# A macaron FFN / Mamba / FFN layer: GpSimd work of the first FFN moved into its down phases, dt * A made by other engines, the short FFN chunk in two matmuls

## The reference, cut to what matters

```python
x = x + 0.5 * ffn(layernorm(x))       # x: (1, 2048, 256)
x = x + mamba(layernorm(x))
x = x + 0.5 * ffn(layernorm(x))       # the same FFN weights

def ffn(x):                           # weights: lut[idx], 16 values
    gate, up = x @ lut[gate_idx].T, x @ lut[up_idx].T     # 256 -> 688
    return (silu(gate) * up) @ lut[down_idx].T            # 688 -> 256

def mamba(h):
    proj = h @ in_proj_w * mup        # z 512, x 512, B 128, C 128, dt 64
    xBC = silu(causal_conv4(xBC) + conv_b)
    dt = softplus(dt + dt_bias)       # 64 heads
    A = -exp(A_log)
    dA = exp(dt * A)                  # the decay of one step
    # scan: state = state*dA + (dt*x) B^T ;  y = C state + D*x
    return (rms_norm(y) * norm_w * silu(z)) @ out_proj_w
```

## Time and profile before

| | |
|---|---|
| runs, us | 550.12, 551.39, 548.0 (median 550.12) |
| profiled execution, us | 552.35, of which the span is 550.6 |
| mean granted PE clock | 0.964 |
| PE busy | 483.1 us, 88% |
| DVE busy | 386.7 us, 70% |
| ACT busy | 280.1 us, 51% |
| POOL busy | 181.0 us, 33% |

### The profile page before, as it was taken

How to read it: one execution, slowest core, us unless ns; L and a number is a source line. 1 busy time by engine, 2 the same in 40 slices (tenths; PEclk the granted TensorE clock), 3 DMA queues, 4 the chain that set the end, 5 groups by cost and what they waited for, 6 DMA issues and landing times.

```text
span 550.6 us, 17195 instructions
## 1 busy us (share of the span) xinstructions
PE 483.1 (88%) x7502; PEld 403.0 (73%) x7502; DVE 386.7 (70%) x734; ACT 280.1 (51%) x506; POOL 181.0 (33%) x229
## 2 busy tenths in 40 slices
PE   4999997989999889548899999999877699999997
PEld 3657886969887678436677778777766678898986
DVE  6998747474749996983687888777758747465542
ACT  3667624232438778766555665556635433232231
POOL 1100006084022221084566667665646311000000
PEclk9999998999999999778899999999989999999999
DMA  9940150000000000010000000000250000101011
GB/s 209 241 166 1 80 245 2 1 1 1 0 1 0 2 0 1 0 38 23 4 4 5 4 5 5 4 4 5 83 249 4 2 3 0 39 1 38 1 39 39
DMA packets 7163, 21.34 MB, mean 39 GB/s; under 512 B 688, under 2 KB 5296, under 8 KB 6448
## 3 DMA queue, kind: packets, MB, share of 16 engines
q1 hardware_dynamic: 6688, 18.08, 9.9%
q10 hardware_dynamic: 400, 2.16, 1.7%
HBM read 12.90 MB, written 6.55 MB: 35 GB/s over the span
## 4 chain that ended last, share of the span: by engine, by line
PE 35%; issue 9%; POOL 5%; DVE 2%; ACT 1%; POOLq 0%; DVEq 0%; ACTq 0%
PE intra L940 4%; POOL w L1169 3%; PE seg L819 3%; PE yo L68 2%; PE yo L70 2%; PE yo L69 2%; PE new L914 2%; PE XB L902 2%; PE XB L873 1%; PE seg L814 1%; PE prior L909 1%; PE intra L68 1%; PE intra L69 1%; PE intra L70 1%; PE yo L889 1%
## 5 line engine op out<-in xcount | busy, mean ns | idle before, releaser
L495 POOL TENSOR_TENSOR n_rstd<-n_ve,m_half 128x4 f32<-128x4 f32 x12 | 13.7, 1145 | 165.6 <-DVE n_ve L491 165.6
L1169 POOL TENSOR_TENSOR w<-xdt,ends 32x512 f32<-32x512 f32 (+3 forms) x63 | 66.5, 1074 | 1.7 <-PE prior L909 1.5
L959 ACT ACTIVATE seg<-seg 128x512 f32<-128x512 f32 x64 | 35.9, 579 | 52.7 <-PE seg L819 52.6
L597 DVE SCALAR_TENSOR_TENSOR cv<-pre,vec,cv 128x512 f32<-128x512 f32 x72 | 59.9, 846 | 3.8 <-ACT cv L653 2.1
L1038 DVE TENSOR_TENSOR mmat<-seg,gs 128x512 f32<-128x512 f32 x64 | 42.5, 684 | 11.8 <-ACT seg L959 11.5
L979 ACT ACTIVATE xbd<-xdt 32x512 f32<-32x512 f32 x64 | 39.9, 624 | 1.2
L819 PEld LDWEIGHTS seg<-abk,m_seg 96*32 96x32 bf16 x2048 | 21.2, 98 | 25.0 <-DVE mmat L1038 14.0
L940 PE MATMUL intra<-xbd,mmat 128*32 128x32 f32 x2048 | 34.3, 223 | 5.0 <-issue 5.0
L940 PEld LDWEIGHTS intra<-xbd,mmat 128*32 128x32 f32 x2048 | 32.0, 152 | 7.8 <-issue 6.0
L68 PE MATMUL pj<-n_xT,win 128*128 128x512 f32 x88 | 35.8, 407 | 1.1 <-PEq L118 1.1
L819 PE MATMUL seg<-abk,m_seg 96*32 96x64 bf16 x2048 | 28.4, 197 | 8.9 <-issue 5.7
(11 more groups left out here) (228 smaller groups left out, 1453.4 us busy)
## 6 DMA issues: line engine op xcount, KB each, us to landing
wgu_dram<-wgu SPq DMA_DIRECT2D x1, 2816.0 KB, 8.2
wgu<-wgu_dram SPq DMA_DIRECT2D x1, 2816.0 KB, 10.5
out<-x_res SPq DMA_DIRECT2D x4, 512.0 KB, 2.9
x_res<-in_x SPq DMA_DIRECT2D x1, 1536.0 KB, 24.4
wd_dram<-wd SPq DMA_DIRECT2D x1, 1536.0 KB, 11.5
wd<-wd_dram SPq DMA_DIRECT2D x1, 1536.0 KB, 13.7
gu_idx<-in_gu ACTq DMA_DIRECT2D x4, 352.0 KB, 8.1
gu_idx<-in_gu SPq DMA_DIRECT2D x4, 352.0 KB, 12.6
```

The lines of the kernel that those rows point to most:

```text
L597: dve.scalar_tensor_tensor(dst, pre[:, x, k:k + GN].rearrange("p (t c) -> p t c", c=P), cw[:, x, k:k + 1], dst, ALU.mult, ALU.add).then_in ...
L959: act.activation(seg[u_ % 2][:, :, :], seg[u_ % 2][:, :, :], ACT.Exp).then_inc(s["exp_ok"], 1)
L1169: pool.tensor_tensor(heads(w[r, n, :]), heads(xdt[a % 2][r, :]), ends[a % 2][r, n * HEADS:(n + 1) * HEADS].unsqueeze(2) .broadcast_to([Q * ...
```

## The change

- `build_masks` no longer sets `m_seg` by a memset and six selections on 32 partitions each; it makes `below = 1 - tri` and one product of two broadcast tiles (96 x 1024).
- GpSimd's steps in the first FFN each wait for `h_lo` of a whole group: masks for group 0, the halves of `win` for groups 1 and 2, `wout` for group 3. The `n_rstd` stand between them.
- Chunk 5 has 48 rows; its low part now goes to partitions 64 to 111 of the high part's tile, and the down weights of chunk 5 stand twice, in both halves of the partitions. Two products per token tile do what three did, in both FFNs. One more copy of 64x256 fills the second half; one memset less clears `hT` and `wd`.
- In the projection's last group A stands by head (one column). ACT multiplies dt by it before the transposes; PE transposes both (16 instead of 8); ACT copies both out and makes the three bf16 parts; DVE makes the two differences. GpSimd has none of it. The softplus steps stand two convolution blocks later on DVE, and the transposes one bank later on PE.

```diff
-    pool.memset(m_seg[:, :, :], 1.0).then_inc(built, 1)
...
-        if b < PARTS:
-            pool.affine_select(out=m_seg[r, :, :], in_=m_seg[r, :, :], compare_op=ALU.is_gt, fill=0.0, base=0,
-                               pattern=[[0, Q], [-1, Q]], channel_multiplier=1).then_inc(built, 1)
...
-            n += 2
         pool.affine_select(out=tri[r, :], in_=tri[r, :], compare_op=ALU.is_ge, fill=0.0, base=0, pattern=[[1, Q]],
                            channel_multiplier=-1).then_inc(built, 1)
         pool.wait_ge(built, n + 1)
         n += 1
+    K = PARTS * Q
+    pool.tensor_scalar(below[:, :], tri[:, :], -1.0, 1.0, ALU.mult, ALU.add).then_inc(built, 1)
+    pool.wait_ge(built, n + 1)
+    pool.tensor_tensor(m_seg[:, :, :], tri[0:K, :].unsqueeze(2).broadcast_to([K, Q, Q]),
+                       below[0:K, :].unsqueeze(1).broadcast_to([K, Q, Q]), ALU.mult).then_inc(built, 1)
+    n += 2
...
+def low_part(hT, c, rows):
+    return hT[0:rows, 1, c, :] if c < FCH - 1 else hT[H64:H64 + rows, 0, c, :]
+def down_mm(pe, out, hT, wd, c, tok):
+    if c < FCH - 1:
+        return split_mm(pe, out, hT[:, 0, c, tok], hT[:, 1, c, tok], wd[:, 0, c, :], wd[:, 1, c, :], c == 0, False)
+    pe.matmul(out, hT[:, 0, c, tok], wd[:, 0, c, :], start=False, stop=False)
+    return pe.matmul(out, hT[:, 0, c, tok], wd[:, 1, c, :], start=False, stop=True)
...
-            for hl in range(2):
-                pool.memset(hT[:, hl, FCH - 1, :].bitcast(F32), 0.0).then_inc(hz, 1)
+            pool.memset(hT[:, 0, FCH - 1, :].bitcast(F32), 0.0).then_inc(hz, 1)
             norm.pool_rstd(pool, 1)
-            norm.pool_rstd(pool, 2)
+            pool.wait_ge(h_lo, FCH)
+            build_masks(pool, T, T["built"])
             for k in range(KC):
+                norm.pool_rstd(pool, k + 2)
+                pool.wait_ge(h_lo, (k + 2) * FCH)
                 pool.wait_ge(split_hi, k + 1)
                 for part in range(4):
                     c = slice(part * PCH * P // 4, (part + 1) * PCH * P // 4)
                     pool.tensor_tensor(win[:, 1, k, :, :].rearrange("p c n -> p (c n)")[:, c], win_raw[:, k, c],
                                        win[:, 0, k, :, :].rearrange("p c n -> p (c n)")[:, c].bitcast(F32), ALU.subtract)
-            norm.pool_rstd(pool, 3)
-            build_masks(pool, T, T["built"])
+            norm.pool_rstd(pool, GROUPS)
+            pool.wait_ge(h_lo, GROUPS * FCH)
             pool.wait_ge(split_hi, KC + 1)
             for k in range(4):
                 pool.tensor_tensor(wout[:, 1, k, :], wout_raw[:, k, :], wout[:, 0, k, :].bitcast(F32), ALU.subtract)
-            norm.pool_rstd(pool, GROUPS)
...
-                    dve.tensor_tensor(hT[0:r, 1, c, :], h[0:r, :], hT[0:r, 0, c, :].bitcast(F32),
+                    dve.tensor_tensor(low_part(hT, c, r), h[0:r, :], hT[0:r, 0, c, :].bitcast(F32),
                                       ALU.subtract).then_inc(h_lo, 1)
...
-                        for e in range(2 if d < FCH - 1 else 1):
-                            ins = act.activation(wd[H64 * e:H64 * e + H64, hl, d, :],
-                                                 down_bank(d)[half, HID * e:HID * e + HID], ACT.Copy)
+                        for e in range(2 if d < FCH - 1 else 2 - hl):
+                            at = HID * e if d < FCH - 1 else 0
+                            ins = act.activation(wd[H64 * e:H64 * e + H64, hl, d, :], down_bank(d)[half, at:at + HID], ACT.Copy)
...
-                    if not ahead and n == 0:
+                    if not ahead and n == 2:
                         dve.wait_ge(eA_ok, 1)
-                        dve.tensor_scalar(A_bc[:, :], A_bc[:, :], -1.0, None, ALU.mult).then_inc(A_ok, 1)
+                        dve.tensor_scalar(A_col[:, :], A_col[:, :], -1.0, None, ALU.mult).then_inc(A_ok, 1)
...
-                    if not ahead and n == 1:
+                    if not ahead and n == 3:
                         dve.wait_ge(nd_ok, 1)
                         dve.wait_ge(ln_ok, 1)
...
+                    if not ahead and n == 5:
+                        dve.wait_ge(hi_ok, 1)
+                        dve.tensor_tensor(rest[:, :], a_tok[:, :], part(0), ALU.subtract).then_inc(rest_ok, 1)
...
+            dve.wait_ge(hi_ok, 2)
+            dve.wait_ge(rest_ok, 1)
+            dve.tensor_tensor(rest[:, :], rest[:, :], part(1), ALU.subtract).then_inc(rest_ok, 1)
...
-            dt_flat = dt_tok[:, :, :].rearrange("p t h -> p (t h)")
-            part = lambda n: ab[:, n, :, :].rearrange("p t h -> p (t h)")
-            pool.wait_ge(dttok_ok, GROUPS)
-            pool.wait_ge(A_ok, 1)
-            pool.tensor_tensor(a_tok[:, :].rearrange("p (t h) -> p t h", h=HEADS), dt_tok[:, :, :],
-                               A_bc[:, :].unsqueeze(1).broadcast_to([P, TILES, HEADS]), ALU.mult).then_inc(a_ok, 1)
-            pool.wait_ge(a_ok, 1)
-            pool.tensor_copy(part(0), a_tok[:, :]).then_inc(hi_ok, 1)
-            pool.wait_ge(hi_ok, 1)
...
-            pool.wait_ge(rest_ok, 2)
-            pool.tensor_copy(part(2), rest[:, :]).then_inc(hi_ok, 1)
...
+                        if last:
+                            act.activation(e, raw, ACT.Abs).then_inc(abs_ok, 1)
                         if g:
                             silu(g - 1, XCH - 1)
-                        if last:
-                            act.activation(e, raw, ACT.Abs).then_inc(abs_ok, 1)
-                            act.wait_ge(abs_ok, 1)
-                            act.activation(e, e, ACT.Exp, scale=-1.0).then_inc(exp_ok, 1)
-                            act.activation(A_bc[:, :], T["a_row"][:, :], ACT.Exp).then_inc(eA_ok, 1)
                     if not last and place == TRANSPOSE_AT + 1:
                         norm.act_hi(act, g + 1)
-                    if last and place == 1:
+                    if last and place == 2:
+                        act.wait_ge(abs_ok, 1)
+                        act.activation(e, e, ACT.Exp, scale=-1.0).then_inc(exp_ok, 1)
+                        act.activation(A_col[:, :], T["a_col"], ACT.Exp).then_inc(eA_ok, 1)
+                    if last and place == 3:
                         act.wait_ge(u_ok, 1)
                         act.activation(ln[:, :], u[:, :], ACT.Ln).then_inc(ln_ok, 1)
+                    if last and place == 4:
+                        act.wait_ge(A_ok, 1)
+                        act.wait_ge(dt_ok, 1)
+                        act.activation(e, raw, ACT.Copy, scale=A_col[:, 0:1]).then_inc(by_head, 1)
                     if last and place == 5:
-                        act.wait_ge(tr_dt, 1)
-                        for q in range(GROUPS):
-                            act.activation(dt_tok[:, q * GT:q * GT + GT, :].rearrange("p (k t) h -> p k t h", k=2),
-                                           pt_dt[:, q * HT:q * HT + HT, :].rearrange("p t (k h) -> p k t h", k=2),
-                                           ACT.Copy).then_inc(dttok_ok, 1)
+                        for n, (out, src) in enumerate(((dt_tok, pt_dt), (a_all, None))):
+                            act.wait_ge(tr_dt, n + 1)
+                            for q in range(GROUPS):
+                                bank_q = src[:, q * HT:q * HT + HT, :] if n == 0 else \
+                                    norm.pt[q // 2][:, q % 2 * HT * P:q % 2 * HT * P + HT * P].rearrange("p (t c) -> p t c", t=HT)
+                                act.activation(by_token(out, q), bank_q.rearrange("p t (k h) -> p k t h", k=2), ACT.Copy
+                                               ).then_inc(a_ok if n else dttok_ok, 1)
+                        act.wait_ge(a_ok, GROUPS)
+                        act.activation(part(0), a_tok[:, :], ACT.Copy).then_inc(hi_ok, 1)
                     if place >= 6:
                         silu(g, place - 6)
+                    if last and place == 6:
+                        act.wait_ge(rest_ok, 1)
+                        act.activation(part(1), rest[:, :], ACT.Copy).then_inc(hi_ok, 1)
             silu(LAST, XCH - 1)
+            act.wait_ge(rest_ok, 2)
+            act.activation(part(2), rest[:, :], ACT.Copy).then_inc(hi_ok, 1)
...
-                    if g == LAST and place == 4:
+                    if g == LAST and place == 5:
                         pe.wait_ge(dt_ok, 1)
                         for t in range(GROUPS * HT):
                             ins = pe.transpose(pt_dt[:, t, :], raw[:, P * t:P * t + P], T["ident"][:, :])
+                        ins.then_inc(tr_dt, 1)
+                        pe.wait_ge(by_head, 1)
+                        pe.wait_ge(norm.lo_ok, 2 * GROUPS * KC + KC)
+                        for t in range(GROUPS * HT):
+                            ins = pe.transpose(norm.pt[t // GT][:, t % GT * P:t % GT * P + P], e[:, P * t:P * t + P],
+                                               T["ident"][:, :])
                         ins.then_inc(tr_dt, 1)
```

60 lines of the change are left out of this document (25 added, 35 removed).

## The result

The changed kernel takes **535.47 us** (median of 4 runs, 532.09 to 536.03) against 550.75 before (4 runs): ratio **0.9729, 95% interval 0.9695 to 0.9763**, 15.3 us less. The forecast was 538.0 in a range of 533.5 to 543.0, faster with a chance of 0.93. Both hold. The sum was short: it had 12.1 us. The profiled execution took 536.03 us (span 534.3), against the 540.25 that the sum gave for it. The timed difference is thus 14.9 us by the ratio (at least 13.0 by its interval); the part on why says where the rest comes from, as far as the runs show it.

The account below looks back on a forecast made before the run. Bounds: GpSimd slowing DVE, so PE waits and loses clock in the first FFN, and the projection's last group. -8.45 - 3.8 + 0.35 - 0.2 = -12.1 us on 552.35 gives 540.25, as a median 538.0; range 533.5 to 543.

Parts of the forecast that it names:

- The sum: Whole kernel: all terms together, -12.1 us, from 552.35 to 540.25 us for the profiled execution.
- The two bounds: First FFN: GpSimd slows DVE and PE waits; projection's last group: GpSimd's chain and ACT's last Silu end together.
- Placement: First FFN, groups 1 and 2: GpSimd's work moved into the down phases saves 8.45 us, bounds -9.35 and -6.0.
- Chunk 5: Down phases of both FFNs: one product less per token tile, 32 x 0.120, saves 3.8 us.
- the +0.35: Ahead of the first down phase: ACT's extra 64x256 copy of down weights costs 0.35 us (0 to 0.4).
- `m_seg`: GpSimd's masks in the first FFN: the one product estimated from the nearest row, 2.94 us.
- Rival 4: First FFN: the broadcast `m_seg` product could be far slower and delay `n_xn`; 556 us at 30 us, chance 0.02.
- The projection's tail: Last projection group: dt * A without GpSimd has all parts ready at 246.5 against 246.79; -0.2 us.
- ACT's chain: Last projection group: ACT works without pause from `dt_ok` to the third cast, 15.3 us.
- the start of the new path: Last projection group: DVE's first block of taps may begin at 219.7 us of the old trace.
- Rival 1: Last projection group: ACT's chain is longer because of handoffs; +2.8 us, 540.8 us, chance 0.14.
- Rival 3: Row products run faster after shorter PE idling, and PE's gaps elsewhere close; -2.6 us, 535.4 us, chance 0.08.

Follow-up runs that it names:

- e2: Kernel before with only GpSimd's first-FFN steps placed in the down phases and `m_seg` as one product; 543.1 us, ratio 0.9847.
- e1: Kernel before with only chunk 5's low half packed and two products, in both FFNs; 547.07 us, ratio 0.9912.
- e4: Kernel before with GpSimd's steps placed in the down phases, but `m_seg` by its memset and six selections as before; 542.85 us, ratio 0.9831.
- e6: Changed kernel with dt * A and its parts done by GpSimd again, as before the change; 537.56 us, ratio 0.9746.
- e10: Kernel before once more, without edit, for a third profile; 549.14 us.
- e3: Kernel before with only dt * A and its three parts taken off GpSimd, softplus steps two blocks later; 547.64 us, ratio 0.9916.
- e8: Changed kernel with 20 products added on PE ahead of its wait for the parts of dt * A; 537.18 us, ratio 0.9767.
- e5: Changed kernel once more, without edit, for a second profile; 537.58 us, ratio 0.9734.
- e7: Changed kernel with all three casts and both differences of dt * A's parts in one row on DVE; 534.59 us, ratio 0.9699.

## Why the prediction was right, and where it was not

**The two bounds it named were the bounds.** The link from GpSimd through `n_xn` and `f_h` to PE's clock went as said, and e2 takes it apart from the rest. Two terms were mis-sized: the tail at the row products, and the scatter of the stages that the change leaves alone.

1. *Placement*, -8.45: measured -8.0 (e2). 0.9 us had been kept back of the full 9.35, and 1.35 are missing; in the changed kernel groups 1 and 2 take 0.41 and 0.68 us more than group 3. That ACT's copies leave them, as the prediction had it, was not isolated.
2. *Chunk 5*, -1.9 in each FFN with +0.35 for a copy: second FFN -1.9 (e1, and the changed kernel). In the first FFN the changed kernel takes 1.8 us less than e2 and e4 from the first `x_res` on, and 1.65 less from group 0's first `n_pt` transpose, where PE waits 0.27 us for the copy: the +0.35 was close. Without the placement e1's one profile got 0.05 of it, which the prediction's separate terms did not foresee. The first FFN as a whole: predicted -10.0, measured 159.45 - 149.79 = -9.7 (-9.8 from the first `x_res` on).
3. *`m_seg`*: estimated from a 2.94 us row, 1.91 measured, and without effect in either form (e4). Rival 4, the slower one, needed 24 us.
4. *The projection's tail*, -0.2 at the row products, 15.3 us of ACT's chain: measured 15.5, so the chain was right. The difference was not: at the row products it is -0.84 to -0.95 against e6 (and the same against e10), and -1.85 in the pair of profiled executions. The step that failed is the start of the new path: it was built on the old times, which contain 1.0 us of the low stretch, and has the first tap of the last group at 219.7 - 159.45 = 60.25 us behind the first projection product, where the changed kernel has 58.8 (208.58 - 149.79). The forecast did not suffer much, by luck: the row products, which the prediction took as before, are 0.5 to 0.7 us longer than e6's, and -0.2 to -0.4 is left at the first `XB`. That 12 us of GpSimd's chain and 6.6 us of DVE's collisions bring only this was the least obvious reading, and it held. Rival 1 (handoffs cost up to 2.8) fell: ACT paused once, 0.28 us. Rival 3 (row products at full clock) did not come in the changed kernel, where PE idled for 5.03 us (4.6 predicted); in e3, after 4.65 us, it came in part (4.09 us). e8 shows that with PE kept busy the products do run at full clock, and that its price was too high: 1.3 us at the first `XB`, not 2.6.
5. *The sum*, -12.1: the stages named give -9.7 - 1.9 - 0.3 = -11.9, and the mean spans of three profiles each, 547.6 and 535.2, differ by 12.4. The timed pairs say more: 14.9 us by the ratio, at least 13.0 by its interval, and e5's repeat of it 0.9734 (at least 11.8). **The term that was missing** is one for the scatter of the stages that the change leaves alone. In the pair of profiled executions, which differ by 16.3 us, it can be read off: 1.6 us of the way to the first `XB` are before's low stretch and 3.0 us the scan, of the same code in both (idle PE, not clock). Taking one execution as the base of a sum puts its own draw of such stretches and waits into the difference, and the prediction allowed 1.7 us for it, where executions of one kernel lie up to 9 apart (before: 546.6 to 555.6 in 33 runs on several chips).

**What stays open**: whether the surplus of some 3 us in the timed runs is more than that draw. For it: by their ratios e1 has 4.9 us (at least 3.0) where its stages show 2.0, e3 4.6 (at least 2.3) where they show 1.1 to 1.3, e4 9.3 and e2 8.5 where 8.0 is shown, and the whole change 14.9 where 11.9 is. But e1 to e4 share one set of 19 runs of the kernel before, the slowest (552.51), so they are not separate witnesses. Against it: the three profiles each; e6, where the part that e3 prices at 4.6 us is worth nothing; and e7 and e8, whose ratios give 16.6 and 12.8 us where the stages give 17.3 and 13.2. A scan that gains about 1 us when GpSimd has no part in dt * A is not excluded: it takes 192.1 us on average in the seven profiles with that part and 190.8 in the six without, a difference within the scatter.
